# Transformer block with attention and a mixture of experts, final stage: loads five tiles ahead, weighted sums of eight tiles on GpSimd, the last sum read from its bank

## The reference

```python
x = x + _layernorm(attn(_layernorm(x)))
h = _layernorm(x)
shared = relu2(h @ shared_up) @ shared_down
a = relu2(einsum('th,ehi->tei', h, w_up)) * combine[:, :, None]     # 2 of 16 experts a token
routed = einsum('tei,eih->th', a, w_down)
x = x + _layernorm(routed + shared)
```

## Time and profile before

| | us |
|---|---|
| median of three runs | 1584.65 |
| lowest and highest of them | 1578.47, 1589.17 |
| the profiled execution, its own time | 1584.75 |
| its span in the trace | 1582.9 |
| mean granted clock of TensorE | 0.982 |
| final stage, first matmul to the end of the span | 1387.5 to 1582.9 |

### The profile page before, as it was taken

The page is one execution under the profiler, slowest core; times in us unless marked ns, Lnnn a source line. Parts: engine busy times, 40 slices in busy tenths (PEclk is TensorE's granted clock), DMA queues, the critical chain, the costliest instruction groups (busy, mean ns, idle before and its releaser), DMA issues.

```text
span 1582.9 us, 21759 instructions
## 1 busy us (share of the span) xinstructions
PE 1500.9 (95%) x7006; PEld 1021.7 (65%) x7006; DVE 975.5 (62%) x1871; ACT 783.9 (50%) x1417; POOL 812.4 (51%) x828
## 2 busy tenths in 40 slices
PE   5699999999999999999998999997999999979997
PEld 3365666656666566666564677785666666658886
DVE  3667677676767676767668437841333333349998
ACT  3255567466575665656647354430222222365554
POOL 1176697777786977769679440013222222043341
PEclk9699999999999999999999999998999999999999
DMA  5869579588595895967953333419977777686773
GB/s 132 139 93 144 90 119 213 73 180 147 89 200 88 147 196 84 176 122 114 236 79 99 133 133 102 158 29 291 293 215 216 218 216 214 224 319 215 232 244 101
DMA packets 162759, 257.76 MB, mean 163 GB/s; under 512 B 20084, under 2 KB 70132, under 8 KB 160596
## 3 DMA queue, kind: packets, MB, share of 16 engines
q1 hardware_dynamic: 144584, 205.12, 57.3%
q0 software_dynamic: 14064, 46.02, 9.9%
q10 hardware_dynamic: 4000, 5.24, 1.0%
HBM read 103.74 MB, written 58.46 MB: 102 GB/s over the span
## 4 chain that ended last, share of the span: by engine, by line
PE 71%; DMA 10%; issue 6%; DVE 4%; POOL 3%; ACT 3%; SPq 2%; another core or an unknown queue 1%; DVEq 0%; POOLq 0%; ACTq 0%
PE bank L113 12%; PE bank L784 8%; PE bank L807 8%; PE bank L716 8%; DMA a<-a 8%; PE bank L624 6%; PE bank L638 6%; PE bank L738 6%; PE bank L643 5%; PE bank L654 5%; POOL a L1597 2%; PE bank L663 2%; PE bank L796 1%; PE bank L581 1%; DMA f<-f 1%
## 5 line engine op out<-in xcount | busy, mean ns | idle before, releaser
L1597 POOL TENSOR_TENSOR a<-a 128x512 f32<-128x512 f32 x384 | 498.6, 1326 | 99.5 <-ACT a L1410 54.1
L1410 ACT ACTIVATE a<-bank 128x512 f32<-128x512 f32 x512 | 296.3, 597 | 258.1 <-PE bank L643 218.6
L917 DVE TENSOR_REDUCE a<-bank 128x1 f32<-128x512 f32 x512 | 321.8, 681 | 79.9 <-PE bank L624 79.2
L113 PE MATMUL bank<-a 128*128 128x512 f32 (+1 forms) x864 | 238.1, 397 | 2.7 <-DVE s L869 1.6
L638 PE MATMUL bank<-a 128*128 128x512 f32 x512 | 217.8, 425 | 5.2 <-ACT a L1410 5.1
L643 PE MATMUL bank<-a 68*128 68x512 f32 x512 | 204.0, 398 | 0.4 <-ACT a L1400 0.2
L624 PE MATMUL bank<-a 128*128 128x512 f32 x512 | 180.6, 424 | 24.4 <-DMA a<-a 20.3
L1665 POOL DMA_INDIRECT f<-h_scratch,f x79 | 76.3, 965 | 229.6 <-DMA f<-f 202.6
L113 PEld LDWEIGHTS bank<-a 128*128 128x128 f32 (+1 forms) x864 | 158.6, 186 | 49.0 <-issue 6.7
L738 PE MATMUL bank<-c 128*128 128x512 f32 x768 | 180.5, 394 | 8.4 <-ACT c L1466 7.4
L716 PE MATMUL bank<-c 128*128 128x512 f32 x768 | 177.5, 390 | 1.5 <-ACT c L1451 1.1
(11 more groups left out here) (187 smaller groups left out, 1776.7 us busy)
## 6 DMA issues: line engine op xcount, KB each, us to landing
a<-a SPq DMA_DIRECT2D x272, 256.0 KB, 9.7
f<-f SPq DMA_DIRECT2D x316, 64.0 KB
yp_scratch<-f SPq DMA_DIRECT2D x79, 256.0 KB
a<-in_L_attn_x SPq DMA_DIRECT2D x15, 1024.0 KB, 11.8
x_scratch<-a SPq DMA_DIRECT2D x8, 1024.0 KB, 4.6
h_scratch<-a SPq DMA_DIRECT2D x8, 1024.0 KB, 13.2
hT_scratch<-s SPq DMA_DIRECT2D x8, 1024.0 KB, 9.9
c<-hT_scratch SPq DMA_DIRECT2D x8, 1024.0 KB
```

The lines of the kernel that those rows point to most:

```text
L113: t = e.matmul(out, a[n], b[n], start=n == 0 and m == 0, stop=n == len(ah) - 1 and m == 2)
L917: e.tensor_reduce(K.mx[:, i, j:j + 1], K.MX[n % 3][:], AX.X, ALU.max).then_inc(Z.max, 1)
L1410: e.activation(K.pt[:, n % NP, :], K.SC[n % 2][:], ACT.Exp, scale=SCALE).then_inc(Z.exp, 1)
L1597: e.tensor_tensor(K.acc[:, j, :], a, K.pt[:, n % NP, :], ALU.add).then_inc(Z.acc, 1)
```

## The change

It has three parts. Loads and gathers are begun five places ahead of use and not eight (`AHEAD`), with `next h` after the first three. The weighted sum of the last eight tiles, ya * g1 + yc * g2, is made by GpSimd in three instructions (`mix`), so that VectorE's `add` has one addition in place of two scaled sums. Tile 31 has no `take`: its `add` reads the bank. In the list the last `rescale` also stands before the last two `finish`.

```diff
+AHEAD = 5
+MIXED = TILES[-8:]
+
+
 def combine_order():
-    out = [("gather", n) for n in range(R)] + [("next h",)]
+    out = [("gather", n) for n in range(3)] + [("next h",)] + [("gather", n) for n in range(3, AHEAD)]
     added, scaled, side = [], [], []
 
     def settle():
         more = []
         for t in scaled:
             more.append(("finish", t))
-            if PLACE[t] + R < NT:
-                more.append(("gather", PLACE[t] + R))
+            n = PLACE[t] + AHEAD
+            if n < NT:
+                more.append(("gather", n))
+            if n - 1 < NT and TILES[n - 1] in MIXED:
+                more.append(("mix", TILES[n - 1]))
...
     def take(b, i):
         added.append(4 * b + i)
-        return [("take", b, i), ("add", 4 * b + i)]
+        return [("take", b, i)] * (4 * b + i < NT - 1) + [("add", 4 * b + i)]
...
-    return out + settle() + settle()
+    last = settle()
+    return out + last[-1:] + last[:-1] + settle()
...
+        self.mix = make("mix_done")
...
-        if t >= EARLY:
+        if t == NT - 1:
+            w.wait_ge(Z.dn, t + 1)
+            w.wait_ge(Z.cs[z], 16 * (n // R))
+        elif t >= EARLY:
             w.wait_ge(Z.so, t + 1)
         else:
             w.wait_ge(Z.cin[z], 16 * LOADS[n])
-        w.wait_ge(Z.cg[z], 32 * (n // R + 1))
-        e.scalar_tensor_tensor(out=sh, in0=K.ya[:, z, :], scalar=K.g1[:, t:t + 1], in1=sh, op0=ALU.mult, op1=ALU.add).then_inc(*csteps.next())
-        w.wait_ge(Z.add, csteps.n)
-        e.scalar_tensor_tensor(out=sh, in0=K.yc[:, z, :], scalar=K.g2[:, t:t + 1], in1=sh, op0=ALU.mult, op1=ALU.add).then_inc(*csteps.next())
+        if t in MIXED:
+            w.wait_ge(Z.mix, MIXED.index(t) + 1)
+            e.tensor_tensor(sh, K.DN[t % 2][:] if t == NT - 1 else sh, K.ya[:, z, :], ALU.add).then_inc(*csteps.next())
+        else:
+            w.wait_ge(Z.cg[z], 32 * (n // R + 1))
+            e.scalar_tensor_tensor(out=sh, in0=K.ya[:, z, :], scalar=K.g1[:, t:t + 1], in1=sh, op0=ALU.mult, op1=ALU.add).then_inc(*csteps.next())
+            w.wait_ge(Z.add, csteps.n)
+            e.scalar_tensor_tensor(out=sh, in0=K.yc[:, z, :], scalar=K.g2[:, t:t + 1], in1=sh, op0=ALU.mult, op1=ALU.add).then_inc(*csteps.next())
...
+    def mix(t):
+        n = PLACE[t]
+        z = n % R
+        ya, yc = K.ya[:, z, :], K.yc[:, z, :]
+        w.wait_ge(Z.cg[z], 32 * (n // R + 1))
+        e.tensor_scalar(ya, ya, K.g1[:, t:t + 1], None, ALU.mult).then_inc(*chain.next())
+        e.tensor_scalar(yc, yc, K.g2[:, t:t + 1], None, ALU.mult).then_inc(*chain.next())
+        w.wait_ge(Z.root, chain.n)
+        e.tensor_tensor(ya, ya, yc, ALU.add).then_inc(Z.mix, 1)
```

More of the change, by code:

```diff
@@ L1686, in gather @@
         e.indirect_dma_start(K.yc[:, z, :], None, K.yp_d, bass.IndirectOffsetOnAxis(K.sl2[:, t:t + 1], 0)).then_inc(Z.cg[z], 16)
-    stages = {"scores": scores, "divide": divide, "root": root, "residual": residual, "split down": split_down, "choose early": choose,
+    def mix(t):
[7 more added lines that the diff above has]
+        e.tensor_tensor(ya, ya, yc, ALU.add).then_inc(Z.mix, 1)
+    stages = {"scores": scores, "divide": divide, "root": root, "residual": residual, "split down": split_down, "choose early": choose, "mix": mix,
               "store": store, "fetch": fetch, "weights": weights, "gather": gather}
```

## The result

The changed kernel takes 1592.93 us (median of 8 runs, 1586.61 to 1597.73), the kernel before 1585.08 (8 runs). The ratio is 1.0038, with a 95% interval of 1.002 to 1.0055: slower by 3 to 9 us, where 1584.0 was forecast. The profiled execution has an own time of 1594.23 us, a span of 1592.2 and a granted clock of 0.982 in the mean.

What follows compares the result with a forecast made beforehand. TensorE, busy 95% of the span, was taken as the bound, leaving only the final stage's head and tail to gain. Loads -1.3, tail -1.6 and mixes +2.2 made -0.7 on 1584.75, so 1584.0 us, range 1574 to 1592.

Steps and rivals of the forecast that it cites:

- The bound: Final stage: TensorE alone bounds it from 1423.5 to 1573.9 us, so time can be saved only at head and tail.
- Loads, -1.3: Head of the final stage: 1.0 MB less traffic ends the full stretch up to 2.6 us sooner; middle taken, -1.3 us.
- ScalarE's unnamed waits: Head: relu at L1480 idle three times, 9.4 us, released by something unnamed; gain only if they end with the traffic.
- Tail, -1.6: After the last matmul: bank addition of 0.69 us and earlier finish save 1.75 us, less 0.15 for the store.
- A mix's price, 2.9 us: GpSimd, last eight tiles: addition 1.33 us, each multiplication between 0.78 and 1.33, nearest the cast; 2.9 us a mix.
- a sign of being wrong: GpSimd's mixes: the prediction called itself wrong if the multiplications take over 1.5 us.
- Blocking, 1.4 us a tile: VectorE beside mixes: four large two-input operations a tile wait for GpSimd's reading, 1.4 us a tile, 5.7 in all.
- Where it falls, four tiles in one half block: Last block's up half: four mixes block 5.7 us, less 2.4 relief and 1.1 room; TensorE waits +2.2 us.
- upper bound 3.7: Last block: TensorE's wait if GpSimd is always reading, 7.2 - 2.4 - 1.1 us.
- Rival 2: Last block: a 3.7 us TensorE wait takes the clock to half, 5 us lost; slower, 1592 us; chance 0.17.
- Rival 1: Last blocks: the mixes cost nothing, TensorE stays dense; 1581.9 us; chance 0.20.
- Rival 3: Head: the stalls go with the lighter transfers and the clock stays up, -10.8 us; 1573.8 us; chance 0.13.

Runs made afterwards that it cites:

- loads_only: Kernel before with only the loads and gathers begun five places ahead, next h after three gathers, no mixes; ratio to the kernel before 0.9997 (0.9983 to 1.0011).
- mix_add: Changed kernel with both multiplications of each mix left out, only GpSimd's addition kept; ratio to the kernel before 1.0036 (1.0023 to 1.005).
- gather3: Kernel before with GpSimd's gathers of places 3 to 7 held until the tile three places earlier is finished; ratio to the kernel before 1.0027 (1.0017 to 1.0037).
- mix_write9: Changed kernel with each mix replaced by nine fills that read nothing; 1578.59 against 1580.32 us for the kernel before, ratio 0.9986.

## Why the prediction was wrong, point by point

- **The bound.** Right: between the head and the tail the change could only lose, and did.
- **Loads, -1.3.** Wrong in size, 0. What failed here is the link from ScalarE's unnamed waits to the transfers' load. With 1 MB less ahead of them the waits were 4.92 and 4.75 us, and in `loads_only` 4.6 and 4.1; on the other chips they are absent, with the same gathers and loads.
- **Tail, -1.6.** Right: the addition from the bank took 0.69 us behind the last matmul, and 7.42 us to the end against 7.4 forecast. It needs the mixes for half of it.
- **A mix's price, 2.9 us.** Wrong: a multiplication is 1.5 to 1.6 us undisturbed and 1.7 in the mean, above both ends of the bounds (0.78 and 1.33). The upper end was taken from an addition of two tensors, as if one input less couldn't cost more. The prediction had named this as a sign of being wrong. Its consequences were small: the last mix ended at 1575.84 rather than 1565, still ahead of its addition at 1584.83, and `mix_add` shows that the loss is there without any multiplication. From start to end a mix took 4.5 to 5.5 us, about the 4.8 that the prediction gave as the limit, and still none was late (L1287 never stood for one). *The statement that one-input GpSimd operations run near line rate (the Trainium skill, GPSIMD Engine Reference, section 4.1) did not hold for it: 1.55 us for 512 elements, more than the 1.29 of the two-input addition.*
- **Blocking, 1.4 us a tile.** Close, in part by luck: 13.2 us over eight tiles, 1.65 each. The prediction counted large operations alone. These lost 7.8 us, 1.0 a tile, and the tiny ones of 128x1, which it put at nothing without a reason, 5.4. *The rule of the Trainium skill (SBUF — State Buffer, "Who interferes with whom") held where these runs test it: two-input rows stretched, one-input statistics did not (694 ns, seven of thirteen of them beside a mix), and fills that read nothing stretched none.* Of the sum from the bank they show nothing, since GpSimd had ended at 1575.84, nine microseconds before it; the rows for that are L944's 0.69 in the earlier trace rows.
- **Where it falls, four tiles in one half block.** This is the step that failed, and the main one. I counted the mixes beside block 7's up half, 5.7 us, and took 2.4 off for three lighter additions. But the mixes began at 1516.64, three tiles and more ahead of that half (which starts at 1534.76), and the first lighter addition came only at 1549.38, five tiles later. Until then each tile had both scaled sums and the blocking, 7.5 us with no relief. The prediction's own date for the first mix, 1521.1, already lay ahead of block 7 (1530.19 in the kernel before). That the mixes began still earlier goes against its sentence that GpSimd's gathers do not move: the first eight didn't, the gather of place 25 came 7 us sooner with the loads five ahead. TensorE's gaps began at 1529.18, ahead of the last step of block 6's down half, and by 1549.27 they were 4.6 us. The later mixes added 5.7 us of blocking, against 0.81 of relief a tile, and 2.1 us of gaps. The forecast was 2.2, its upper bound 3.7, measured 6.7 in named gaps and 7.8 for the stretch.
- **Rival 2** came nearest in time (1592) but not by its mechanism: six waits of up to 2.3 us took no clock with them (1.00 throughout), where it had 5 us of half clock. (In `gather3` waits of 0.7 and 2.7 us were followed by 3.4 us at 0.50.)
- **Rival 1** is what a mix that reads nothing does: `mix_write9`, 1.7 us faster. **Rival 3** didn't happen.

The sum by measured terms: 0 for the loads, -1.65 for the tail, +7.8 for the blocks, makes +6.2 on 1585.08, 1591.3; the ratio's interval is +3 to +9 us. The remaining 3.1 us between the two profiled spans, 0.8 ahead of the stage and 2.3 in the head, belong to no part of the change that the runs could name: heads of 55.6 to 58.1 fall on kernels with and without each part. On the third chip the parts close, 138.44 - 131.21 - 1.65 = 5.6 us, against medians 5.5 apart.

## What to carry to other kernels

Work moved from VectorE to GpSimd is not free because GpSimd is idle: count VectorE's two-input operations beside it as blocked, the tiny ones too (here 1.3 us a tile for one addition of 1.3, and 1.65 for a mix of 4.8), and compare this with what VectorE saves (here 0.81 a tile). Then date both: the blocking starts with the first moved instruction, the saving only when its result is used, and with a buffer of several tiles between, the stretch in the middle has the cost without the gain. And a price that no row shows should not be bounded from above by an operation that merely looks heavier.

## What the runs showed of the hardware

- Where nothing stretches it, GpSimd's multiplication of a 128x512 tile by a column or by a constant takes 1.48 to 1.6 us, more than its addition of two such tiles (1.29); a fill of that size takes 0.47 to 0.53.
- A blocked VectorE operation of 128x1 can wait as long as one of 128x512: 1.93 us for 0.16 in `mix_add`. It began 0.61 us ahead of the row of GpSimd's addition and ended with it, while another indirect DMA issue still stood in GpSimd's row; whether the engine held something by then, or the rows are rough there, is open.
- The same kernel differs by 7 us (1579.75 to 1586.94) from one chip and occasion to another, and the final stage's head by 8 to 9 (55.6 and 47.7, 57.9 and 48.6), by waits of ScalarE whose cause the profile can't name.
- Waits of TensorE of 1.3, 2.3, 1.0, 0.5, 0.5 and 1.1 us within 39 us left its granted clock at 1.00; in `gather3` waits of 0.7 and 2.7 us, 5.6 us apart, were followed by 3.4 us at 0.50.
